# New orders for the steps of five engines in a two-layer macaron block, without filler products

## What is computed

```python
x = x + 0.5 * _L0_ffn_ref(_layernorm(x), ...)      # 128 -> 512 -> 128, ternary weights, two norms
x = x + _L0_attn_ref(_layernorm(x), ...)           # one scan over 512 steps, 16 states
x = x + 0.5 * _L0_ffn_ref(_layernorm(x), ...)
x = x + 0.5 * _L1_ffn_ref(_layernorm(x), ...)      # top 2 of 8 experts: 128->256->64->(8x128)->64->256->128
x = x + _L1_attn_ref(_layernorm(x), ...)           # 256 channels x 16 states, scan in chunks of 32
x = x + 0.5 * _L1_ffn_ref(_layernorm(x), ...)      # the mixture once more, same weights
```

```python
def step(carry, inp):
    a, bu, c = inp
    carry = a * carry + bu
    y = jnp.einsum('bkdn,bkn->bkd', carry, c)
    return (carry, y)
```

## Time and profile before

| | |
|---|---|
| median of 3 runs | 1121.41 us |
| the runs | 1113.58 to 1122.65 us |
| span of the profiled execution | 1116.6 us |
| TensorE (PE) busy | 935.0 us, 84% |
| VectorE (DVE) busy | 762.5 us, 68% |
| ScalarE (ACT) busy | 659.4 us, 59% |
| GpSimd (POOL) busy | 515.7 us, 46% |
| mean granted TensorE clock | 0.933 |

### The profile page before, as it was taken

The page is one execution under the profiler, slowest core; times in us unless marked ns, Lnnn a source line. Parts: engine busy times, 40 slices in busy tenths (PEclk is TensorE's granted clock), DMA queues, the critical chain, the costliest instruction groups (busy, mean ns, idle before and its releaser), DMA issues.

```text
span 1116.6 us, 11275 instructions
## 1 busy us (share of the span) xinstructions
PE 935.0 (84%) x3446; PEld 451.9 (40%) x3446; DVE 762.5 (68%) x1717; ACT 659.4 (59%) x1030; POOL 515.7 (46%) x413
## 2 busy tenths in 40 slices
...
GB/s 136 10 1 86 1 54 249 143 132 48 246 120 164 73 229 130 167 158 210 86 181 96 227 180 163 92 172 208 142 123 136 202 108 206 119 270 134 142 86 9
DMA packets 44717, 151.83 MB, mean 136 GB/s; under 512 B 4464, under 2 KB 12784, under 8 KB 40560
## 3 DMA queue, kind: packets, MB, share of 16 engines
...
...
## 4 chain that ended last, share of the span: by engine, by line
PE 46%; DVE 25%; ACT 14%; issue 6%; POOL 6%; DMA 2%; SPq 0%; DVEq 0%; POOLq 0%; ACTq 0%
DVE dA L982 11%; PE yp L1483 9%; ACT L116 5%; PE mp L1442 5%; PE pp L1362 4%; PE mp L1427 3%; PE fp L1264 3%; PE fp L1248 3%; PE pp L1228 3%; DVE hs L989 3%; ACT dA L1207 2%; PE mp L1451 2%; POOL dbu L708 2%; PE mp L1228 2%; PE pp L1332 1%
## 5 line engine op out<-in xcount | busy, mean ns | idle before, releaser
L708 POOL TENSOR_TENSOR dbu<-du,b_row 128x1024 f32<-128x1024 f32 x128 | 301.2, 2356 | 178.8 <-DVE dA L982 176.9
L982 DVE TENSOR_TENSOR_SCAN dA<-dA,dbu 128x512 f32<-128x512 f32 x256 | 312.4, 1220 | 75.5 <-ACT dA L1207 41.5
L1483 PE MATMUL yp<-hs,ident 128*128 128x512 f32 x512 | 273.1, 636 | 58.2 <-DVE hs L989 57.7
L1207 ACT ACTIVATE dA<-delta,pr 128x512 f32<-128x512 f32 x256 | 173.8, 686 | 104.3 <-DVE hs L989 103.1
L989 DVE TENSOR_TENSOR hs<-dA,c_row 128x512 f32<-128x512 f32 x256 | 177.0, 691 | 28.1 <-PE yp L1483 18.2
L116 ACT ACT_TABLE_LOAD x130 | 166.8, 1283 | 15.0 <-POOL delta L639 11.4
L1483 PEld LDWEIGHTS yp<-hs,ident 128*128 128x128 f32 x512 | 89.7, 196 | 169.4 <-DVE hs L989 101.7
L1427 PE MATMUL mp<-cont,ex_ 64*128 64x512 f32 x128 | 75.5, 671 | 15.5 <-DVE he L940 11.6
L1431 PE MATMUL mp<-cont,ex_ 64*128 64x512 f32 x128 | 75.6, 672 | 3.2 <-DVE he L945 3.2
L1248 PE MATMUL fp<-sq,w 128*128 128x512 f32 x128 | 71.1, 679 | 5.7 <-ACT sq L1030 4.1
L1264 PEld LDWEIGHTS fp<-w,hT 128*128 128x128 f32 x512 | 63.5, 193 | 29.2 <-issue 14.1
...
## 6 DMA issues: line engine op xcount, KB each, us to landing
b_row<-held SPq DMA_DIRECT2D x104, 512.0 KB, 4.9
c_row<-held SPq DMA_DIRECT2D x104, 512.0 KB, 4.1
...
```

Of the source, the lines that this page charges most:

```text
L708: pool.tensor_tensor(out=dbu[:, j % 2, :].rearrange("p (r t) -> p r t", r=2), in0=d, in1=b_n, op=ALU.mult).then_inc(dbu_r.sem, 1)
L982: dve.tensor_tensor_scan(out=dA[:, half], data0=dA[:, half], data1=dbu[:, j % 2, half], initial=0.0, op0=ALU.mult, op1=ALU.add).then_inc(h ...
L1207: act.activation(out=dA[:, r * SEQ:(r + 1) * SEQ], in_=delta[:, i % 2, c, :], func=ACT.Exp, scale=mA[:, c, 2 * k + r:2 * k + r + 1]).then_ ...
L1483: pe.matmul(yp[:, :], lhsT=ident[:, :], rhs=hs[:, j % 2, r * SEQ:(r + 1) * SEQ], start=(s % PAIRS == 0 and r == 0), stop=(s % PAIRS == PAI ...
```

## The change

Each of the five strings in `ORDER` is replaced. The threads, their steps and the number of steps of each letter stay as they are, but for K, which is gone with its generator, its tile of zeros and the memset that filled it. Two waits change place or are new: ScalarE's S step asks for its table before it waits for `start_r`, and GpSimd's multiplication into `dg` (from the second mixture pass on) waits until GpSimd's own addition of the pass before has ended, the one that reads `dg`.

The order strings cut to the first lines of ScalarE and TensorE, and all that isn't an order string:

```diff
     "ACT":
-        "FFPFFFFFFFFFFFFFFFFFFFFFFFPFPFFPFFPFFPFPPPFFFFFEEEFFEFPFFPFFFPFPPPPFPFPFFSSFSPSFSPSFFPSSFPSSPSPSSPSS"
-        "FSFSSFFSFSSEFSEESFSSFFSSEFFSFFPSFSPSSPFPFPFPFFPFFPFPFSSSPSSSPSPPSPSFSSFPFPSSFSSFSSSFFSFFSSESFEESSFSF"
...
+        "FFFFPFFFFFFFFFFFFFFFFFFFFFPFPFFPFFFPFPFPPPFFFFFEEEFFFFEFFFFPFPPFPFPFPFFPFPFPFFSSPPSPSSPPSFPPSFSSSFSF"
+        "FSSSESFESESFSFFFEFSFFSPSPSSFSPSSPPSSPSSPPFPSSFFPFSPFFPFFSSPSFSPSPPSSSSFFSFFSFSSESEEFSSFSFFEFFFSFSPFS"
...
     "PE":
-        "PFEPFEFFFFFFFFFFFFFFFFFFFFFFFFPFPFFPFFPFPEFFPPPKKKKEKFEFEEEFEFEKKFFKFPFPFFFPFFPPPKPFPFKKFFSSKPSFSFPS"
-        "FPSFPSSFKPESSSPSKSKSFSFSESEFSEFEESESFSESFFSFSSSSFFFSPFFPSSSPFSPFPFPFPFFPFFFSKKSPSSPSPSPSEPSFSFPSPSSF"
...
+        "PFFFFFFFFFFFFFFFFEFFFFFFPFFFFPFPFFEPFFPFPEFFPPEFEFEEFFEEEFFFFFPFFPFFPPFPFPFPFPFPFFFFPSPPPSPSSPSFSSFE"
+        "SSSEFEFESSEESESFSESFFFSSFSPFFPSSFFPPSPSSSPSPPFSSFSFSPFSPFSFPFSPFSPFSSPSSSEPSFSFSEESEFFEESESEFSFSSFFS"
...
-FILL = 256
...
-        zeros = sb("zeros", [P, P])
...
-            ch.add(pool.memset(zeros[:, :], 0.0))
...
                 x, ready, n = layer_input(m)
                 yield True
                 pool.wait_ge(ddr.sem, ddr.at(m, 1))
+                if m >= 1:
+                    stage, i = M_TURNS[m - 1]
+                    added = hx_new if stage == "moef" else xo_new
+                    pool.wait_ge(added.sem, added.at(i, 1))
                 pool.tensor_tensor(out=dg[:, :, :], in0=dd, in1=all_tiles(mlng), op=ALU.mult).then_inc(dgr.sem, 1)
...
                             yield True
+                            table(ACT.Exp)
                             if h % (2 * STEPS) == 0:
                                 act.wait_ge(start_r.sem, start_r.at(i, 1))
-                            table(ACT.Exp)
...
-            def k_thread():
-                order = ORDER["PE"]
-                for at in (n for n, name in enumerate(order) if name == "K"):
-                    yield True
-                    alone = order[:at].count("S") in (0, 2 * BATCH * STEPS)
-                    pe.matmul(yp[:, 0:FILL], lhsT=zeros[:, :], rhs=w1[:, 0:FILL], start=alone, stop=alone,
-                              skip_group_check=True)
-
-            side_by_side(ORDER["PE"], F=f_thread(), P=p_thread(), E=e_thread(), S=s_thread(), K=k_thread())
+            side_by_side(ORDER["PE"], F=f_thread(), P=p_thread(), E=e_thread(), S=s_thread())
```

More of the change, by code:

```diff
@@ L39 @@
     "SP":
-        "AGGGABBBBBBBBBBBBBBBBBGGBAGBBBBBBBBBBBBBBBBBBBBBABBBBBGGGBBBBBBBBBBBBBBBBBBBBBBABBBBGBGGBGGGBBBBBBBB"
-        "BDBBBBBBBBBBBBBBBBBGAGGGGGBBBBBBBBBBDBBBBBBBBBBBBBBBBGGABGBGGGBBBBBBBBBDBBBBBBBBBBBBBBBBGBGGGBGBGBBB"
-        "BBBBBDBBBBBBBBBBBBBBBBGBGGGBGBGBBBBBBBBDBBBBBBBBBBBBBBBBBGGGBBBBBBBGBBGGBDDGGGD",
+        "AGGGABBBBBBBBBBBBBGBGBGBBBBBBBBBABBBBBBBBBBBBBBBGGBAGBBBBBBBBBBBBBBBBBBBBBBBBBGBGGBBBBBGGGBABBBBBBBB"
+        "BBBBBBBBBBBGBBGBGBBABBBGDGGBBBBBBBBBBBBBBBBBBBBGGGBBBBDBBGGAGBBBBBBBBBBBBBBBGBGBBBBBGGBBDBGBBGBBBBBB"
@@ L43 @@
+        "BBBBBBBBBBBBBBBGGGBBBBBGDBBGGBBBBBBBBBBBBBBBBBBBBBBBBBBGGGBDBBBBBBBBBBGGGDGGGDD",
     "Pool":
-        "PFEFFFFFFFFFPFPFPFFFEEFEPPFFPSSPFSPSSSSFSFSFSSFSFSSEESEPPSFFFPSSPSPFSSFSFSSSSFSSSFEESESPFFSPFPSSPFSP"
-        "SSFPSPSSFSFSFEESEPSSPSSEESEFFFPSSPSPSSSFSPPFSSFSFFEEEPSPSSSSSEEEFFFPSPSPSSSSPSPFSSFFSSSFEEFEPPSSSEES"
-        "EFFPSPFSSPSSSPFSPSFSFSSFSEEFESPSPSSEEEFPSPSSSSSPSPSSPSSEEESPPSSSSEEEPSPSPSSSSSSPSPSSSSEESESSPPEEEEEE",
+        "FPFEFFFFFFFFPFFFFFFEEPEPPPFFFPPSSFSFSSFSSSFPSSEEEPSSSFPFSSSFFPPSSSSFSFSFSFSSPFEEESPSSSFFSSPFSPPSPSSS"
@@ L47 @@
+        "SPFSFPSSFSEEFESPSFSSFPSFSPSPPSSESFEFPSPFSSESFSSEEFESPFSSPSSFSPPFSSEESPSFPSSFFFSESSPSFEFEEPSSSFSSFSPP"
+        "PSEEPSPSFSFFSFSESFSEEPESPSSSFSFSSSPPPSSPSPSESSPSEESSSSEEESPSSSSSPPPSSSSSESESSESSPPSPSSSSEESEPEEEPEEE",
     "DVE":
-        "FEFFPEFFFFFFFFFFPPPFFPFEEEEEEEEFFFEPFFFPSSSSSSSSSSSPPFSFSFSSSEESSEESEFEESFEFSSSSSESSSPSSSFSFFPSSFSSS"
-        "SSFSFSSSPPSSSPSSFSEEFSEEFEESSESSESSSSESSSPSFSFFPSSSSSFSSSSSSFSFSSPPPSSSSEESEEFEESEFPPEFSPSSESEESPEES"
-        "EESEESSSSSSESSFSFFPSSSSSSSSSSSSFSPPPFSFSSEESSEESEEPEEPFFFPSSESEESPEESEESEESSSSSSSESSSFFFPSSSSSSSSSSS"
@@ L51 @@
-        "PPPSFSSSFSFEESPPEESEEPEESSFSSFSFEEESEESPEESEESSSSSSESSSFFFSPSSSSSSSSSPPPFSSSFFSSEEPPEESEEPSEFSESSFSF"
-        "SESEESSPEESEESEESSSSSSESSFFPSSSSSSSSSSSPPPSSSSSEEEEEEPPEEPSSSSESESEPPEESEESSEESSSSSSESSSSSSSSSSSSSPP"
-        "SSSPSPSEESEESSEESEESSSSPPSSESSSSSESESEESEESEEPPEPPEEEEEEEEE",
-    "ACT":
-        "FFPFFFFFFFFFFFFFFFFFFFFFFFPFPFFPFFPFFPFPPPFFFFFEEEFFEFPFFPFFFPFPPPPFPFPFFSSFSPSFSPSFFPSSFPSSPSPSSPSS"
-        "FSFSSFFSFSSEFSEESFSSFFSSEFFSFFPSFSPSSPFPFPFPFFPFFPFPFSSSPSSSPSPPSPSFSSFPFPSSFSSFSSSFFSFFSSESFEESSFSF"
[L57 to L61, removed]
@@ L62 @@
-    "PE":
-        "PFEPFEFFFFFFFFFFFFFFFFFFFFFFFFPFPFFPFFPFPEFFPPPKKKKEKFEFEEEFEFEKKFFKFPFPFFFPFFPPPKPFPFKKFFSSKPSFSFPS"
-        "FPSFPSSFKPESSSPSKSKSFSFSESEFSEFEESESFSESFFSFSSSSFFFSPFFPSSSPFSPFPFPFPFFPFFFSKKSPSSPSPSPSEPSFSFPSPSSF"
[L65 to L70, removed]
+        "FFEFPFFFFFFFFFFPEPPFFFPEEEEEEEEFFFEPFFFPFSSSFFSSPPSSSSSEESEEFEESEFSEFSSSESSSPSSSSSSSFFSFSSSSPSSSSSSS"
@@ new lines @@
+        "SPPFSSFFSSSSEEEEEEFESFEFSSSSEPSSSPSSSSFSSFFSSSSSSSPSSSSSSSSPPPSFSFFSSEESEEPPEESESEFSSSPFEFSSPSSESSES"
+        "SSFSFSFSSSEEEEEEPSSSESSSSFSPPPFSFSSSEESEESEESESPESSPSFESFFPSSPSSSSESESSEESSEFEFPEESSFSSSSESSSPPSPSSS"
+        "SFSFFESEPEEPSEESEEFSSSFFSESPESSPESESESSSSFSFFESSEEPSSSSESSEPPPSSSSFSFEFESEEPEEPSESSEFSSFFSESSSPPSSSS"
+        "ESESSSFSFEESESESSEPSESSSSSSSSEPPPSSSSSEESSSEEPEEPEESSSSSSPESSSSPSSSSSESESSEESSESESEPSESSSSSSSSSPPESS"
+        "SSSEESEESPEESEEPSSSSSSSSSSSPPSESSSSEESEESEEPEPPPEEEEEEEEEEE",
```

13 lines of the change are left out of this document (added).

## The result

The changed kernel takes 1064.09 us (median of 4 runs, 1060.31 to 1069.35), the kernel before 1121.22 us beside it: ratio 0.951, 95% interval 0.946 to 0.955. The forecast was 1095, with a range down to 1066. The direction was right and the gain, 57 us, more than twice the 26 that were forecast. The profiled execution was the longest of the four, 1069.35 us with a span of 1067.6.

A forecast was written before the change was run, and what follows sets the result against it. No single bound: waits between engines matter, with scans dense inside rows and stopping between them. Terms -27 - 2.6 + 0 - 4 + 7 + 3 - 3 = -26.6 on 1116.6 give 1090, plus 4.8 is 1095 us; 8-in-10 range 1066 to 1136.

The forecast's parts named there:

- The holes close: The seven gaps between rows of scans shrink to 5 us each, so 65.5 us of hole go.
- The payback: Work leaving the holes goes into the rows and costs 38 us there, leaving net -27 us.
- Rival B: The work only moves: 65.5 us return inside the rows, VectorE waiting for the FFN; 1122 us, chance 0.21.
- The fillers: 44 TensorE products, 18.57 us, leave: -4 us for their time, +7 us for one more clock fall.
- rival C: Without fillers TensorE's clock falls in more places, up to 7.3 us each; slower by over 1%, chance 0.17.
- Table loads: On ScalarE, 124 loads instead of 130, six of 1.283 us, a third counted: -2.6 us.
- The moved table call: ScalarE's load ahead of the start wait saves at most eight loads, 10.3 us; put at 0, covered by `dbu`.
- the new GpSimd wait: GpSimd waits for its own previous addition: 0, at most 1.27 us each in the last two places.
- `b_row`: B and C spill and broadcasts may come last in the holes: 0, at most 4.9 us in each of seven.
- The start: Five more ScalarE steps and two table loads ahead of the first scan: +3 us, ends 0 and 6.7.
- The tail: Last MoE pass but one: three TensorE steps move behind the last front; -3 us, ends -7.3 and +7.2.
- The base: Profiled span of 1116.6 us, plus the 4.8 us by which the median of the runs lies above it.

## Why the forecast fell short

**The holes close: right, and nearly sized.** 56.1 us instead of 65.5. I took 5 us for each remaining hole; 44.4 us were left. Hole 0/1 keeps 9.6 us because another wait came last in it (TensorE's last addition), and in hole 4/5 VectorE is busy for 8.84 of 10.18 us, so that one isn't a gap any more. VectorE's idle time in holes went from 83.2 to 23.4 us. The forecast named the FFN wait of the earlier trace rows and, for rows 3 to 6, `du`; the trace shows the end of `du` ahead of the next scan by the same 2.7 to 2.8 us at all seven boundaries.

**The payback: the step that failed.** The forecast took the work that leaves the holes for work that comes into the rows, priced it by each engine's density, weighed the three prices by the engines' shares of the chain, and came to +38 us; the rows show -1.6. Both the amounts and the prices were too large.

*The amounts.* By the earlier trace rows and the sum of the windows above, VectorE has 1.1 us more work in the rows, not 7.5, since its holes kept 20.9 us. ScalarE has 14.0 more, not 35: of the 33 us that left its holes 7.7 went ahead of the first scan, 7.7 went away as table loads, and 4 are not accounted for. TensorE has 7.2 more, or some 26 if the 18.57 us of fillers are taken out of the old rows, not 44; only 35 us left its holes. In the forecast's own sum 1.1, 26 and 14.0 give 20 us.

*The prices.* Measured, a microsecond costs 0.6 to 1.0 on VectorE, 0.2 on TensorE and 0.3 on ScalarE. On the forecast's amounts that is 24 to 27 us; on the amounts that came, 10. A share of the chain says how often an engine comes last, not what a microsecond more on it costs; and that an engine is 64% or 90% busy doesn't make it the one that paces.

What took the last 10 us, to -1.6, is not isolated. The fillers that left the old rows are worth some 4 us at TensorE's measured price. The rest can be the clock: the same rows took 776.9 us in the second profile of the changed kernel and 784.2 in that with tail fillers beside it, at 0.98 and 0.96 (in this order):

```profile
169.84:991.68 821.84, 742.31 (x2694) 343.64 (x2694) 701.03 (x1441) 549.13 (x859) 464.63 (x329) 0.98 0.49 170
```

```profile
170.28:998.88 828.60, 751.12 (x2694) 346.70 (x2694) 701.60 (x1441) 549.27 (x858) 464.55 (x329) 0.96 0.49 168
```

Against the old orders without fillers, at 0.93, the new rows are 6.3 us shorter. That the clock explains this is argued, not shown.

**Rival B** (the work only moves) read the earlier trace rows as 70.9 us that stand beside scans. Only 28.1 of them stood in holes; 42.7 lay ahead of the first scan. Where the old holes held 28.1, the new rows hold 4.0, and the rest stands ahead of the first scan: the order did not move this wait into the rows.

**The fillers and rival C: a wrong part, then undone.** The forecast put the fillers at -4 for their time and +7 for one further fall of the clock, net +3. In the old orders leaving them out costs 7 us at a lower clock, as C has it. In the new orders the clock between the scans doesn't fall; that this is because the holes are shorter is argued, not shown. In the tail it did fall in the profiled execution (0.53 from 1020 to 1030 us), and hardly in the second profile. The two parts of the change aren't independent, and a sum of separate terms couldn't see that.

**Table loads**: six fewer, as counted; at the measured 0.3 the 7.7 us are worth 2.4, against 2.6 forecast. **The moved table call and the new GpSimd wait**: the first measured at 0 within the scatter. The kernel without the new wait wasn't tried. **`b_row`**, put at 0 with 34 us as its end, did come late: GpSimd waits 17.7 us for it, but the scans wait only 4.6 us for `dbu`, so it held them up directly for 4.6 us at most. **The start**: +1.9 in the profile, +3 forecast. **The tail**: +6.8 in one execution and -3.4 in another, -3 forecast; it scatters by 10 us with the clock, so one execution says little about it.

**The base** was a small miss as well: the profiled span lies 1.75 us below its own run's time in the changed kernel, so of the 4.8 us added to the span most was scatter between runs.

In sum: the forecast of -27 for holes less payback was -58 by the table, and everything else together came to +9 in the profiled execution and to about nothing in others.
